# ScalarE evicts the second layer's state in unit 4s+4, ahead of squares and field copy, in place of unit 4s+5 (interaction network, one core, Trainium2)

## Chip, cores and metric

One Trainium2 chip, one core. The metric is the device time of one execution in microseconds (us). The engines named below are TensorE (PE: matmuls; PEld: its weight loads), VectorE (DVE), ScalarE (ACT), GpSimd (POOL) and SyncE (SP, which here only issues DMAs).

## What is computed

The kernel looks up 32 embeddings of 16 numbers for each of 2048 samples, passes them through three layers of a compressed interaction network, and puts the sums of the three layers and 16 dense numbers through a small MLP. Cut to what matters:

```python
e = stack([tbl_f[ids[:, f]] for f in range(32)], axis=1)          # (2048, 32, 16): x0
xk = x0
for W in (W0, W1, W2):                                            # (32, 32|64, 64)
    xk = relu(einsum('bmd,bhd,mhk->bkd', x0, xk, W))              # x1, x2, x3: (2048, 64, 16)
    outs.append(sum(xk, axis=2))
h = concatenate(outs + [dense_ctx], axis=1)                       # 208 wide
h = relu(h @ W_top1 + b_top1); h = relu(h @ W_top2 + b_top2)
y = h @ W_top3
```

## The kernel before, in words

**Blocks, pairs, units.** The 2048 x 16 pairs of sample and dimension are 32768 columns, cut into 64 blocks of 512 columns (s = 0 to 63). Two blocks make a pair (p = 0 to 31). Layers 1 and 2 of a block (from x1 to x2, and from x2 to x3) are contracted over 32 fields times 64 states, which is 16 matmul steps of 128 rows; four steps are one unit, so a block has four units, 4s to 4s+3, and a pair eight. An fp32 matmul stands in the trace as two instructions.

**The main loop.** Every engine runs the same loop, `for n in range(262)`, with four places i = 0 to 3 inside each n. In this document "unit n" is what an engine does for that n, and (n, i) is a place in it. The order of each engine's work is written out by hand and is fixed; engines meet through semaphores only, and each engine does its own list strictly in order.

- VectorE (`products`, line 637) makes at unit n first P1(n), the product of the loaded fields with x1 for layer 1, then P2(n-6), the product of the same fields with x2 for layer 2. P1 has three buffers, P2 two: P2(m) waits until TensorE has done P2(m-2), which is at TensorE's unit m+4. P2(4s), the first product of a block, also waits for x2 of block s (the semaphore `s_x[2]`). P2(4s) is made at VectorE's unit 4s+6.
- TensorE (`contract`, line 759, matmuls at L775) does at each place of unit n one step of P1(n) into the lower half of the array's columns and one of P2(n-6) into the upper half. Between the steps it does other work by tables: `sum_fields` (L698, L705) of the next pair into the one PSUM tile `wide`, `l0_tile` (L729), which multiplies the squares by the first layer's weights, `turn` (L681), which turns the next pair's fields round, and the MLP in `piece`s (L786, L795, L805).
- ScalarE evicts. `take_x2(s)` (line 476) waits for two things: TensorE's unit 4s+3 of layer 1, and P2(4s-1), the last reader of the x2 of the block before (`xp[2]` is one buffer). It then writes relu of the accumulator twice into `xp[2]` (L487, two instructions) and once into `zin` (L492). `square(p, t)` (line 444) squares what `sum_fields(p, t)` left in `wide` (L454); for t = 0 it first copies the fields (L452), and afterwards issues the DMA that stores them to DRAM (L458).
- SP (`keep_rows`, line 250) loads each unit's fields from DRAM, broadcast over partitions, into ten buffers `kept`; the loads of unit n wait for P2(n-10), and those of a pair also for its stored fields.

**The tables around the change.** For pairs from p = 3 on (p = 4 has two other places), the places are these, counted from unit 8(p-1):

```python
    SUMS_AT[later] = [(0, 2) if later == 4 else (0, 0), (1, 1), (2, 2), (4, 0), (4, 3)]
    L0_AT[later] = [(3, 0), (3, 2), (4, 2), (5, 0), (5, 2)]
```

So TensorE does the five tiles of field sums at (0,0), (1,1), (2,2), (4,0) and (4,3) of every eight units, and ScalarE has its squares of the same tiles at the same places of its list. There is one PSUM tile `wide` for all of them: `sum_fields(p, t)` waits (semaphore `s_took`) until ScalarE has squared tile t-1. At unit 8(p-1), ScalarE's list has, for t = 0, the copy of fields, the square and the store; then, at unit 8(p-1)+1, `take_x2` of an odd block, ahead of the square of t = 1. At unit 8(p-1)+4 it has the square of t = 3 at place 0 and that of t = 4 at place 3; then, at unit 8(p-1)+5, `take_x2` of an even block.

**MLP pieces.** Nine pieces for each group of four sample tiles are done at place 2 of units 79, 81, 87, 89, 95, 97, 103, 105, 111, then 64 units later, and again 64 units later; a last group is done near the end. Eight pieces of a group are eight matmul instructions each, the ninth is the small last layer.

Of the kernel before, what the change touches and what calls it, by code (L numbers as in the profile page):

```python
# [18 lines left out]
BLOCKS = B * D // BLK  # L19
# [6 lines left out]
UNITS = BLOCKS * GT  # L26
OFF = 6
# [24 lines left out]
def places(table):  # L52

    at = {}
    for p, where in table.items():
        for t, (o, i) in enumerate(where if isinstance(where, list) else [where]):
            at[8 * (p - 1) + o, i] = (p, t)
    return at


TURNS, SUMS, L0S, X1S = (places(table) for table in (TURN_AT, SUMS_AT, L0_AT, X1_AT))

SPLIT_AT = {1: (9, 10), 2: (4, 5)}
# [24 lines left out]
def halved(layer, s):  # L88

    return (layer, s) in ((1, 0), (2, BLOCKS - 1))  # L90


def tower(nc, dense_t, ids, tables, w_top1, b_top1, w_top2, b_top2, w_top3, w0_pairs, w0_all, w1, w2,
          sel_sums, identity, x0_rows, out):
    with ExitStack() as ctx:
# [299 lines left out]
        def _(act):  # L395
# [34 lines left out]
            def split_high(t):  # L430
                tile0 = M - EARLY if t % 2 == 0 else M
                act.wait_ge(s_gather[t % 2], 16 * (tile0 + M * (t // 2)))
                nc.scalar.copy(parts[:, :, 0, :], emb[t % 2][:, :, :].rearrange("p m d -> p d m"))\  # L433
                    .then_inc(s_high, 1)

            def split_mid(t):
                act.wait_ge(s_rest, t)
                nc.scalar.copy(parts[:, :, 1, :], rest[:, :, :]).then_inc(s_mid, 1)

            def take_x0(p):  # L440
                act.wait_ge(s_wide, 6 * (p - 1) + 1)
                nc.scalar.copy(x0[p % 2][:, :, :], wide[:, :, :]).then_inc(s_took, 1)  # L442

            def square(p, t):
                k = ST * p + t
                if k >= 2:
                    act.wait_ge(s_l0, k - 1)
                act.wait_ge(s_wide, 6 * (p - 1) + 2 + t)
                if t == 0:
                    if p >= 2:  # L450
                        act.wait_ge(s_stored[p % 2], 16 * (p // 2))
                    nc.scalar.copy(fields[p % 2], wide[0:M, :, :]).then_inc(s_fields, 1)  # L452
                n = 2 if t < ST - 1 else 1
                nc.scalar.activation(sq[k % 2][:, 0:n, :], wide[:, 0:n, :], ACT.Square).then_inc(s_took, 1)  # L454
                if t == 0:

                    act.wait_ge(s_fields, p)
                    act.dma_start(x0_rows[p].rearrange("j m n -> m j n"), fields[p % 2])\  # L458
                        .then_inc(s_stored[p % 2], 16)

            def take_x1(s):
                j = s % 2
                act.wait_ge(s_l0, ST * (s // 2 + 1))
                if s:
                    act.wait_ge(s_prod[1], 4 * s)
                src = acc0[64 * j:64 * j + 64, :]
                nc.scalar.activation(xp[1][0:64, :], src, ACT.Relu)  # L467
                nc.scalar.activation(xp[1][64:128, :], src, ACT.Relu).then_inc(s_x[1], 1)
                if s == 0:
                    for b in range(GT, rows):  # L470
                        keep_made(b)
                if s >= 6:
                    act.wait_ge(s_z12, (s - 6) // 4 + 1)
                nc.scalar.activation(zin[0:64, s % 6, :], src, ACT.Relu).then_inc(s_xz[1], 1)

            def take_x2(s):
                act.wait_ge(s_done[1], 4 * s + 4)
                if s:
                    act.wait_ge(s_prod[2], 4 * s)
                if halved(1, s):  # L480
                    src = [(accs[64 * c:64 * c + 64, s % 2, 0:HALF], slice(HALF * c, HALF * c + HALF))
                           for c in range(2)]
                else:
                    src = [(accs[0:64, s % 2, :], slice(0, BLK))]
                for half in range(2):
                    for bank, cols in src:
                        last = nc.scalar.activation(xp[2][64 * half:64 * half + 64, cols], bank, ACT.Relu)  # L487
                last.then_inc(s_x[2], 1)
                if s >= 6:
                    act.wait_ge(s_z12, (s - 6) // 4 + 1)  # L490
                for bank, cols in src:
                    last = nc.scalar.activation(zin[64:128, s % 6, cols], bank, ACT.Relu)  # L492
                last.then_inc(s_xz[2], 1)

            def take_x3(s):
                act.wait_ge(s_done[2], 4 * s + 4)
                if s >= 4:
                    act.wait_ge(s_z3, s // 4)
                if halved(2, s):
                    for c in range(2):  # L500
                        last = nc.scalar.activation(x3[:, s % 4, HALF * c:HALF * c + HALF],
                                                    accs[64 * c:64 * c + 64, s % 2, 0:HALF], ACT.Relu)
                else:
                    last = nc.scalar.activation(x3[:, s % 4, :], accs[64:128, s % 2, :], ACT.Relu)  # L504
                last.then_inc(s_xz[3], 1)

            def take_event(g, e):
                first, tiles = GROUPS[g]
                n = tiles * NB
                act.wait_ge(s_ev, 7 * g + e + 1)  # L510
                if e < 4:
                    nc.scalar.activation(h1[:, e, 0:n], exch[:, 0:n], ACT.Relu).then_inc(s_taken, 1)
                elif e < 6:
                    nc.scalar.activation(h2[:, e - 4, 0:n], exch[:, 0:n], ACT.Relu,
                                         bias=bt2[:, e - 4:e - 3]).then_inc(s_taken, 1)
                else:
                    nc.scalar.copy(y[:, first:first + tiles], exch[:, 0:tiles]).then_inc(s_taken, 1)
                if e == 3 and g + 2 < len(GROUPS):
                    load_dense(g + 2)
# [31 lines left out]
            for n in range(LAST):  # L551
                for i in range(GT):
                    t = n // 16 + 1
                    if i == 1 and t < BT and n % 16 == SPLIT_AT[t][0]:
                        split_high(t)
                    if i == 1 and t < BT and n % 16 == SPLIT_AT[t][1]:
                        split_mid(t)
                    if n % 4 == (OFF - 1) % 4 and i == 0 and 0 <= n - OFF + 1 < UNITS:
                        take_x2((n - OFF + 1) // 4)
                    if n % 4 == (OFF + 4) % 4 and i == 0 and n >= OFF + 4:  # L560
                        take_x3((n - OFF - 4) // 4)
                    if (n, i) in TURNS:
                        take_x0(TURNS[n, i][0])
                    if (n, i) in SUMS:
                        square(*SUMS[n, i])
                    if n % 8 == 2 and i == 0 and n + 2 < UNITS:
                        take_x1((n + 2) // 4)
                    if (n, i) in X1S:
                        take_x1(2 * X1S[n, i][0])
                    if (n, i) in PIECES_AT:  # L570
                        g, q = PIECES_AT[n, i]
                        if q < 4 or q == 8:
                            take_event(g, min(q, 6))
                        elif q % 2:
                            take_event(g, 4 + (q - 4) // 2)
# [367 lines left out]
```

## Time and profile before

| | |
|---|---|
| runs of the kernel before | 1278.5, 1280.6, 1282.85 us; median 1280.6 us |
| the profiled execution | span 1334.7 us from the first to the last instruction; the profile gives no other time of its own |
| TensorE busy | 92% of the span |
| VectorE busy | 86% |
| ScalarE busy | 39% |
| GpSimd busy | 51% |
| granted TensorE clock, mean | 0.990 of 2.4 GHz |

A row of a timeline gives the start in us from the span's start, the duration in us, engine, line, operation, output tile <- input tiles with partitions x elements and type, and how many instructions are merged. The bracket at the end is how long the engine was idle before the row and what released it. VectorE's and TensorE's instructions overlap a little with the next ones, so a product of 2.28 us duration is followed by the next 2.20 us after its start. In VectorE's rows, `prod<-kept,xp` is a P1 and `prod<-kept,xe` a P2 (x2 lies in the PSUM tile `xe`). In TensorE's rows, `prod,w1s` is layer 1 and `prod,w2s` layer 2.

### The profile page before, as it was taken

What the parts mean: (1) busy time and instruction counts of PE and PEld (TensorE: products, weight loads), DVE (VectorE), ACT (ScalarE), POOL (GpSimd) and SP (SyncE); (2) the same over time, 40 slices, a digit from 0 to 9 for tenths busy, and PEclk for the clock granted to TensorE, in tenths of its full rate; (3) what the DMA queues carried; (4) which work ended last, traced back from release to release, by engine and by line L of the source; (5) the groups of instructions that cost most, each with busy time, mean ns of one, the idle gap of its engine ahead of it and who ended that gap; (6) DMA issues with size and microseconds to landing.
All of it is one profiled execution on the core that took longest, in us unless ns stands there. A gap on an engine that the chain in (4) does not pass through costs nothing.

```text
span 1334.7 us, 16080 instructions
## 1 busy us (share of the span) xinstructions
PE 1233.3 (92%) x6140; PEld 507.4 (38%) x6140; DVE 1150.9 (86%) x534; ACT 517.9 (39%) x758; POOL 684.3 (51%) x705
## 2 busy tenths in 40 slices
PE   0779698999999999999999899999999999999998
PEld 0332233433444433333443333333444433333444
DVE  3259588989989899999998899999999999999994
ACT  0334143434434344444334344334434344434421
POOL 6553666674866556463745456374655652020201
PEclk9989899999999999999999999999999999999999
DMA  5348577997878788888899999999999988777850
GB/s 115 100 109 215 142 224 201 218 223 218 244 214 239 216 249 221 232 224 229 235 190 206 213 233 230 237 232 228 229 243 247 241 238 225 226 221 224 229 155 1
DMA packets 73547, 277.45 MB, mean 208 GB/s; under 512 B 29752, under 2 KB 38619, under 8 KB 41183
## 3 DMA queue, kind: packets, MB, share of 16 engines
q1 hardware_dynamic: 54324, 267.09, 77.3%
q0 software_dynamic: 16384, 4.23, 3.1%
q10 hardware_dynamic: 2762, 5.12, 1.5%
q8 instruction: 48, 0.79, 0.3%
q14 instruction: 29, 0.23, 0.1%
HBM read 272.15 MB, written 4.20 MB: 207 GB/s over the span
## 4 chain that ended last, share of the span: by engine, by line
PE 52%; DVE 15%; issue 12%; DMA 9%; another core or an unknown queue 4%; ACT 3%; POOL 2%; SPq 2%; DVEq 0%; ACTq 0%; POOLq 0%
PE accs L775 37%; DVE prod L649 15%; DMA kept<-x_rows 9%; PE acc L729 6%; PE wide L698 2%; POOL emb L293 2%; SPq L256 2%; PE xe L786 2%; PE xe L795 2%; ACT xe L487 1%; PE wide L681 1%; ACT sq L454 0%; PE accs L771 0%; ACT x3f L452 0%
## 5 line engine op out<-in xcount | busy, mean ns | idle before, releaser
L775 PE MATMUL accs<-prod,w2s 128*64 128x512 f32 x2016 | 950.6, 597 | 27.8 <-DVE prod L649 19.1
L775 PE MATMUL accs<-prod,w1s 128*64 128x512 f32 x2016 | 940.2, 596 | 0.0
L649 DVE TENSOR_TENSOR prod<-kept,xe 128x2048 f32<-128x2048 f32 x256 | 584.2, 2283 | 98.2 <-ACT xe L487 37.0
L293 POOL DMA_INDIRECT emb<-in_tbl,idx x512 | 485.9, 949 | 261.1 <-issue 123.0
L649 DVE TENSOR_TENSOR prod<-kept,xp 128x2048 f32<-128x2048 f32 x256 | 583.9, 2282 | 31.4 <-issue 13.8
L775 PEld LDWEIGHTS accs<-prod,w1s 128*64 128x64 f32 x2016 | 270.3, 137 | 266.4 <-issue 236.1
L775 PEld LDWEIGHTS accs<-prod,w2s 128*64 128x64 f32 x2016 | 266.1, 137 | 264.3 <-issue 185.0
L454 ACT ACTIVATE sq<-wide 128x1024 f32<-128x1024 f32 (+1 forms) x155 | 145.7, 940 | 310.4 <-PE wide L698 78.7
L729 PE MATMUL acc<-sq,u 128*64 128x512 f32 x640 | 234.1, 597 | 10.0 <-ACT sq L454 9.8
L698 PE MATMUL wide<-x,sums 128*64 128x512 bf16 x500 | 107.3, 384 | 11.7 <-issue 6.9
L332 POOL TENSOR_TENSOR x3f<-x3f 64x512 f32<-64x512 f32 x31 | 39.7, 1279 | 133.1 <-ACT x3f L504 132.9
L729 PEld LDWEIGHTS acc<-sq,u 128*64 128x64 f32 x640 | 67.4, 138 | 90.6 <-issue 71.9
L300 POOL TENSOR_TENSOR rest<-emb,parts 128x512 f32<-128x512 f32 x15 | 21.3, 1423 | 121.6 <-ACT parts L433 121.6
L487 ACT ACTIVATE xe<-accs 64x512 f32<-64x512 f32 (+1 forms) x130 | 73.1, 562 | 24.4 <-DVE prod L649 18.6
L312 POOL TENSOR_TENSOR zin<-zin 128x512 f32<-128x512 f32 x32 | 41.2, 1287 | 77.3 <-ACT zin L492 75.6
L504 ACT ACTIVATE x3f<-accs 64x512 f32<-64x512 f32 x63 | 37.5, 595 | 100.1 <-PE accs L775 74.9
L442 ACT CAST x<-wide 128x1024 bf16<-128x1024 f32 x31 | 31.4, 1012 | 103.2 <-PE wide L681 78.5
L698 PEld LDWEIGHTS wide<-x,sums 128*64 128x64 bf16 x500 | 39.9, 110 | 70.5 <-issue 59.5
L452 ACT COPY x3f<-wide 32x1024 f32<-32x1024 f32 x31 | 31.0, 1001 | 83.5 <-PE wide L698 57.6
L467 ACT ACTIVATE xp<-acc 64x512 f32<-64x512 f32 x64 | 36.4, 569 | 63.0 <-DVE prod L649 46.0
L842 PE MATMUL acc<-u 128*128 128x384 f32 x32 | 12.9, 564 | 35.6 <-DMA emb<-in_tbl,idx 35.6
L492 ACT ACTIVATE zin<-accs 64x512 f32<-64x512 f32 (+1 forms) x65 | 37.9, 584 | 1.6
(85 smaller groups left out, 463.1 us busy)
## 6 DMA issues: line engine op xcount, KB each, us to landing
kept<-x_rows SPq DMA_DIRECT2D x252, 512.0 KB
kept<-x_rows SPq DMA_DIRECT2D x504, 256.0 KB
emb<-in_tbl,idx POOLq DMA_INDIRECT x512
x_rows<-x3f ACTq DMA_DIRECT2D x31, 128.0 KB
prod<-in_w_all ACTq DMA_DIRECT2D x1, 512.0 KB, 6.2
w1s<-in_L_rec_W SPq DMA_DIRECT2D x4, 128.0 KB
w2s<-in_L_rec_W SPq DMA_DIRECT2D x4, 128.0 KB
wt<-in_W_top SPq DMA_DIRECT2D x1, 512.0 KB
```

The lines of the kernel that those rows point to most:

```text
L293: pool.indirect_dma_start(emb[t % 2][:, m, :], None, tables[m], bass.IndirectOffsetOnAxis(ap=idx[:, t, m:m + 1].bitcast(U32), axis=0)).the ...
L312: pool.tensor_tensor(zin[:, a, :], zin[:, a, :], zin[:, a + 1, :], ALU.add).then_inc(s_zp, 1)
L332: pool.tensor_tensor(x3[:, a, :], x3[:, a, :], x3[:, a + 1, :], ALU.add).then_inc(s_z3p, 1)
L454: nc.scalar.activation(sq[k % 2][:, 0:n, :], wide[:, 0:n, :], ACT.Square).then_inc(s_took, 1)
L467: nc.scalar.activation(xp[1][0:64, :], src, ACT.Relu)
L487: last = nc.scalar.activation(xp[2][64 * half:64 * half + 64, cols], bank, ACT.Relu)
L492: last = nc.scalar.activation(zin[64:128, s % 6, cols], bank, ACT.Relu)
L504: last = nc.scalar.activation(x3[:, s % 4, :], accs[64:128, s % 2, :], ACT.Relu)
L649: nc.vector.tensor_tensor(prod[layer][:, q % BUFS[layer], :, :], kept[:, q % KEPT, :, :], xp[layer][:, :].unsqueeze(1).to_broadcast([128, ...
L698: last = mm(bank[64 * c:64 * c + 64, :], sums[:, t, 64 * c:64 * c + 64], x0[p % 2][:, j, :], start=True, stop=True)
L729: last = mm(acc0[64 * j:64 * j + 64, :], w, squares, start=t == 0, stop=t == ST - 1)
L775: last = mm(accs[64 * (layer - 1):64 * layer, s % 2, :], wk[layer][:, t, :], prod[layer][:, q % BUFS[layer], i, :], start=t == 0, stop=t = ...
```

## The change

On ScalarE, `take_x2(s)` moves from place (4s+5, 0) to unit 4s+4: for an odd s to place 0, where it stands ahead of the copy of fields and the square of tile 0; for an even s to place 3, ahead of the square of tile 4 and behind that of tile 3. Nothing is added or taken away, and no other engine's list is touched.

```diff
+X2S = {(4 * s + 4, 0 if s % 2 else 3): s for s in range(BLOCKS)}
 TURNS, SUMS, L0S, X1S = (places(table) for table in (TURN_AT, SUMS_AT, L0_AT, X1_AT))
...
-                    if n % 4 == (OFF - 1) % 4 and i == 0 and 0 <= n - OFF + 1 < UNITS:
-                        take_x2((n - OFF + 1) // 4)
+                    if (n, i) in X2S:
+                        take_x2(X2S[n, i])
                     if n % 4 == (OFF + 4) % 4 and i == 0 and n >= OFF + 4:
                         take_x3((n - OFF - 4) // 4)
                     if (n, i) in TURNS:
```

## Rows read from the trace of the kernel before

**Rows 1.** The profile page, busy us (share of span) and instructions of two engines.

```profile
PE 1233.3 (92%) x6140; PEld 507.4 (38%) x6140; DVE 1150.9 (86%) x534; ACT 517.9 (39%) x758; POOL 684.3 (51%) x705
```

**Rows 2.** Groups by line, VectorE's P2: busy us, mean ns | idle before, by releaser.

```profile
L649 DVE TENSOR_TENSOR prod<-kept,xe 128x2048 f32<-128x2048 f32 x256 | 584.2, 2283 | 98.2 <-ACT xe L487 37.0 <-remote 27.3 <-issue 20.1
```

**Rows 3.** VectorE's timeline, a pair without MLP pieces: P2(112), P2(115), P2(117), P2(120).

```profile
651.91 2.29 DVE L649 TENSOR_TENSOR prod<-kept,xe 128x2048 f32<-128x2048 f32 x1 [1.27 <-issue]
...
665.11 2.28 DVE L649 TENSOR_TENSOR prod<-kept,xe 128x2048 f32<-128x2048 f32 x1
...
673.90 2.28 DVE L649 TENSOR_TENSOR prod<-kept,xe 128x2048 f32<-128x2048 f32 x1
...
688.44 2.29 DVE L649 TENSOR_TENSOR prod<-kept,xe 128x2048 f32<-128x2048 f32 x1 [1.27 <-issue]
```

**Rows 4.** ScalarE's timeline in the same pair, blocks 29 and 30.

```profile
664.63 1.00 ACT L452 COPY x3f<-wide 32x1024 f32<-32x1024 f32 x1 [2.45 <-issue]
665.65 1.02 ACT L454 ACTIVATE sq<-wide 128x1024 f32<-128x1024 f32 x1
...
667.48 1.15 ACT L487 ACTIVATE xe<-accs 64x512 f32<-64x512 f32 x2 [0.80 <-issue]
668.65 0.59 ACT L492 ACTIVATE zin<-accs 64x512 f32<-64x512 f32 x1
...
686.63 0.60 ACT L454 ACTIVATE sq<-wide 128x512 f32<-128x512 f32 x1 [2.62 <-PE wide L705]
687.25 1.15 ACT L487 ACTIVATE xe<-accs 64x512 f32<-64x512 f32 x2
```

**Rows 5.** VectorE's timeline, a pair with MLP pieces: P2(96), P2(101), P2(104).

```profile
577.28 2.29 DVE L649 TENSOR_TENSOR prod<-kept,xe 128x2048 f32<-128x2048 f32 x1 [2.28 <-ACT xe L487]
...
599.60 2.29 DVE L649 TENSOR_TENSOR prod<-kept,xe 128x2048 f32<-128x2048 f32 x1 [0.26 <-PE accs L775]
...
615.39 2.29 DVE L649 TENSOR_TENSOR prod<-kept,xe 128x2048 f32<-128x2048 f32 x1 [2.29 <-ACT xe L487]
```

**Rows 6.** TensorE's timeline, same pair: starts of units 104, 106, 110, 111, and work between.

```profile
589.91 0.59 PE L775 MATMUL accs<-prod,w1s 128*64 128x512 f32 x1
...
595.49 0.60 PE L698 MATMUL wide<-x,sums 128*64 128x512 bf16 x4
...
596.78 1.89 PE L795 MATMUL xe<-h,wt 128*64 128x512 f32 x8
598.50 0.59 PE L775 MATMUL accs<-prod,w1s 128*64 128x512 f32 x1
...
599.36 0.59 PE L775 MATMUL accs<-prod,w1s 128*64 128x512 f32 x1
...
618.46 0.59 PE L775 MATMUL accs<-prod,w1s 128*64 128x512 f32 x1
...
621.90 0.59 PE L775 MATMUL accs<-prod,w1s 128*64 128x512 f32 x1
622.12 0.64 PE L775 MATMUL accs<-prod,w2s 128*64 128x512 f32 x1
```

**Rows 7.** ScalarE's timeline near the start: a square that TensorE's field sums wait for.

```profile
87.15 1.02 ACT L454 ACTIVATE sq<-wide 128x1024 f32<-128x1024 f32 x1
```

**Rows 8.** TensorE's timeline, two early places: field sums that waited for a square.

```profile
88.23 0.62 PE L698 MATMUL wide<-x,sums 128*64 128x512 bf16 x4 [2.04 <-ACT sq L454]
...
228.00 0.64 PE L705 MATMUL wide<-x,sums 128*64 128x512 bf16 x2 [3.52 <-ACT sq L454]
```

**Rows 9.** TensorE's timeline, pair without pieces: field sums of tile 1.

```profile
668.41 0.59 PE L698 MATMUL wide<-x,sums 128*64 128x512 bf16 x2
```

**Rows 10.** Chain of waits, 655 to 700 us: a unit's loads on the path, start, us.

```profile
681.81 13.32 DMA kept<-x_rows
```

**Rows 11.** Stretches behind both waits: PE, PEld, DVE, ACT, POOL, granted clock, DMA.

```profile
88.30:92.00 3.70, 3.70 (x16) 1.33 (x17) 2.42 (x2) 1.03 (x1) 2.60 (x3) 1.00 0.50 95
227.50:231.00 3.50, 3.00 (x9) 1.34 (x11) 3.50 (x2) 2.65 (x5) 0.00 (x0) 0.51 0.19 70
```

## Prediction, made before the change was run

> **What bounds the kernel now.** I read the page's busy shares first: TensorE 1233.3 us and VectorE 1150.9 us of a 1334.7 us span [rows 1]. Two engines are nearly full, so a wait of one matters only where the other is not the bound at that moment. Then the groups by line: VectorE's idle time stands before its P2 products, 98.2 us, and the largest named releaser is the eviction of x2 (37.0 us) [rows 2]. Then the timelines, pair by pair, because the answer differs by stage.
>
> In a pair **without MLP pieces**, P2 of an even block starts late once per eight units: P2(112) and P2(120) each stand behind an idle of 1.27 us, 36.53 us apart [rows 3]. Between them VectorE is back to back: ten products from 651.91 to 673.90, 2.20 us each [rows 3]. Sixteen such products would be 35.2 us. The cause of the late one is on ScalarE: x2 of block 30 starts at 687.25, straight behind the square of tile 4 (686.63 and 0.60 long), and that square had waited for TensorE [rows 4]. The odd block shows no wait on VectorE, and its x2 had nothing to do with a square: after the square ended at 666.67 ScalarE stood idle 0.80 us and began x2 at 667.48, which is 0.09 after P2(115) ended (665.11 + 2.28) [rows 3, 4]. x2 of an odd block is released by P2(4s-1), and no place in the list can make it earlier.
>
> In a pair **with MLP pieces** the idle before P2(104) is 2.29 us, and P2(96) and P2(104) are 38.11 us apart [rows 5]. Here TensorE is the bound: its starts follow each other without a gap in its lower columns, and the only trace of VectorE's lateness is the upper half of unit 111, 0.22 us behind the lower (622.12 against 621.90) [rows 6]. A P2 even waits for TensorE, 0.26 us [rows 5].
>
> **The change part by part.** Three instructions of ScalarE (two relus to `xe`, one to `zin`) move; their number and durations stay. What counts is what stands behind what.
>
> *Even blocks: the gain.* x2 now stands behind the square of tile 3 and needs P2(4s-1) only; it is written while VectorE makes P1(4s+6), 2.20 us, and takes 0.09 + 1.15 us. The idle before P2(4s) goes: 1.27 us in a pair without pieces [rows 3]. The square of tile 4, now behind it, still waits for TensorE's sums (idle 2.62 before it) [rows 4], so it costs nothing; if that cover went, it would be late by 1.76 us. In a pair with pieces only the 0.22 us of rows 6 can come back; the rest of the 2.29 becomes waiting for TensorE.
>
> *Odd blocks: the cost.* x2 now stands ahead of the copy and square of tile 0, and it waits for P2(4s-1), in the middle of the unit. The copy, the square and the store's issue queue behind that wait, and TensorE's sums of tile 1 wait for the square. From the start of P2(4s-1): product 2.28, release 0.09, relus to x2 1.17, zin 0.62 (its 0.59 and the step to the next), copy 1.02, square 1.02 [rows 3, 4], release of TensorE 0.06 (88.17 to 88.23) [rows 7, 8]: **6.26 us**. In the pair of rows 3 that is 665.11 + 6.26 = 671.37, where TensorE did these sums at 668.41 [rows 9]: it stops for about 2.9 us the first time. The store is issued 4.6 us later; between its issue (behind the square at 665.65) and the next pair's first load (the loads on the chain begin to count at 681.81) there are now 15 us, then some 10. The trace shows no landing for it; the bounds are nothing and that of the far larger loads, 13.32 us [rows 10], which would make loads 3 us late per pair. I take nothing, as the store is an eighth of the bytes, and keep the other end as a small chance.
>
> *Pairs without pieces, summed.* The stop feeds the next wait. TensorE has, after the sums of tile 1, the rest of that unit and four units. By rows 6 the rest is 599.36 - 595.49 less the piece (598.50 - 596.78 = 1.72), 2.15, and units 106 to 109 are 618.46 - 599.36 = 19.10. Then VectorE's P2 that needs the last of them starts 0.24 later (599.60 against 599.36) [rows 5, 6], and four products at 2.20 lead to the next P2(4s-1). Round: 6.26 + 2.15 + 19.10 + 0.24 + 8.80 = **36.55 us**, against 36.53 now. The gain is all given back: VectorE no longer waits for ScalarE at P2(4s), but for TensorE at the P2s behind it. Bounds: 35.2, if TensorE made the stop up by itself, and 36.53 + 2.9, if nothing of the 1.27 helped.
>
> *Pairs with pieces, summed.* TensorE is the bound, and P2(4s-1) is released by the end of its unit 4s+3: start of unit 104 (589.91) + 0.24 + 6.26 = 596.41, against 595.49 now [rows 6]. It stops 0.92 us per pair and gets back 0.22: **+0.70 us**, 38.8 for 38.11. (The same round by VectorE, 36.55 + 1.72 = 38.27, is shorter, so TensorE's holds.) Bounds: -0.22 and +1.24, the latter if P2(4s-1) stays at VectorE's present pace.
>
> *Elsewhere.* In the first two pairs no square stands at the moved place; the end has no squares at all. Nothing.
>
> *Sum.* Of the pairs from p = 3 on, twelve are as rows 5 (three groups of pieces, four each): 12 x 0.70 = 8.4. Some sixteen are as rows 3: 16 x 0.02 = 0.3. Together about **+8.7 us**: the profiled execution 1334.7 to 1343.4, the median 1280.6 to 1289.3. The profiled execution is 54 us longer than the median; it has idle stretches in its first third with other releasers (27.3 us "remote" before P2 alone [rows 2]). I take the regular pairs as the common part and add the difference to the median: **1289 us**.
>
> **The clock.** The stop in pairs without pieces is in the steady round 36.55 less what TensorE needs: 38.11 - 0.22 - 2 x 1.72 = 34.45, so about 2.1 us. A wait of 2.04 us for a square left the granted clock at 1.00 (2.4 GHz); one of 3.52 us was followed by 3.5 us at 0.51, so near 1.2 GHz [rows 8, 11]. Ours lies with the first row, and I count nothing. The Trainium skill, "TensorE: Matmul & The Clock Gate", Part 1, says that the array falls to half clock after idling and earns the full one back by sustained work; the second row agrees. By that rule, if it bit here, the sum would be the one of the third rival below.
>
> **The rivals.**
> 1. *The gain stays* (faster). TensorE makes up the stop, and VectorE alone sets pairs without pieces: 16 x (36.53 - 35.2) = 21 us, and 12 x 0.22 = 3 with pieces: 1257 us. It decides at TensorE's sums of tile 1: if the square is taken by the time it gets there, or if TensorE has 2 us to spare per pair. For it: 36.53 - 34.45 = 2.1 us of room today, and 0.75 at 35.2. Against it: the stop falls in front of the units with the most extra work, and pieces leave no room. Half the gain would be about 1269. Chance 0.11.
> 2. *It cancels* (same). The stop in pairs with pieces is partly hidden, say a release to x2 before P2(4s-1)'s profiled end, or a zin and copy that overlap more: at 0.6 us less per pair 1282. Chance 0.15. That the change does nothing for odd blocks (their x2 cannot start earlier) is already in the sum.
> 3. *The clock falls* at the stops: a drop costs half of 3.5 us, 1.7; sixteen pairs: 27 more, 1316. Or late stores, 3 us in some pairs, toward 1310. For it: the first stop of 2.9 us lies between the two rows; against it: the steady one does not. Chance 0.07.
>
> **How the numbers follow.** The forecast (slower, about 1289) has 0.67. Its own range is 1284.5 to 1296: twelve pairs at up to 1.24, sixteen at up to 0.05 either way or a little over. A measurement of this kernel can tell about 0.3%, 3.8 us, from no change. The range that should hold 8 in 10 takes in the cancelling case and stops short of the gain and of the clock: 1279 to 1297. Slower 0.67 + 0.07 = 0.74; same 0.15; faster 0.11.
>
> **What would show it.** In the changed profile: no idle of 1.27 or 2.29 before P2 of even blocks; instead P2s that wait for TensorE by some tenths; TensorE idle before L698, released by the square L454, about 2 us in pairs without pieces and 0.9 with; x2 of odd blocks unmoved, 0.09 after P2(4s-1), then zin, copy and square in a row; pairs 36.5 and 38.8 us long. I am wrong if TensorE does not wait before L698, if pairs without pieces come out near 35.2, or if the granted clock shows 0.5 in the steady part.

## The result, and the profile after the change

The changed kernel takes 1301.86 us (median of four runs, 1300.65 to 1306.82) against 1281.72 us before (four runs, 1278.5 to 1282.92) in the same comparison: the ratio is 1.0167, 95% interval 1.0137 to 1.0198. It is slower by 20 us, where the forecast said 9 and its range ended at 1297. The direction held, the size did not.

The page of the changed kernel, then its P2 group and its P1 group (its lines stand one lower than before: L650 for L649, L699 for L698, L488 for L487):

```profile
PE 1212.2 (93%) x6140; PEld 438.1 (34%) x6140; DVE 1153.5 (88%) x534; ACT 515.8 (40%) x758; POOL 682.9 (52%) x705
```

```profile
L650 DVE TENSOR_TENSOR prod<-kept,xe 128x2048 f32<-128x2048 f32 x256 | 584.5, 2284 | 87.8 <-PE accs L776 77.7 <-ACT xe L488 7.1 <-issue 0.3
L650 DVE TENSOR_TENSOR prod<-kept,xp 128x2048 f32<-128x2048 f32 x256 | 583.5, 2281 | 10.5 <-ACT xp L469 10.5
```

Against [rows 2], the eviction of x2 no longer stands first among the releasers of P2; TensorE does, with 77.7 of 87.8 us. That is the exchange that the forecast described: the old wait is gone and another engine's lateness has its place.

The timeline of VectorE in two pairs without MLP pieces, to be held against [rows 3] (P2(112), P2(113), P2(115), P2(121), P2(129)):

```profile
620.55 2.29 DVE L650 TENSOR_TENSOR prod<-kept,xe 128x2048 f32<-128x2048 f32 x1 [0.31 <-PE accs L776]
...
625.84 2.29 DVE L650 TENSOR_TENSOR prod<-kept,xe 128x2048 f32<-128x2048 f32 x1 [0.81 <-PE accs L776]
...
634.64 2.28 DVE L650 TENSOR_TENSOR prod<-kept,xe 128x2048 f32<-128x2048 f32 x1
...
662.42 2.29 DVE L650 TENSOR_TENSOR prod<-kept,xe 128x2048 f32<-128x2048 f32 x1 [0.81 <-PE accs L776]
...
700.70 2.29 DVE L650 TENSOR_TENSOR prod<-kept,xe 128x2048 f32<-128x2048 f32 x1 [0.81 <-PE accs L776]
```

The idle of 1.27 before the even block's first product has become 0.31, released by TensorE, and P2(113) waits 0.81 more. From P2(113) to the same product of the next pair is 662.42 - 625.84 = 36.58 us.

ScalarE in that pair, against [rows 4], and TensorE's sums of tile 1, against [rows 9]:

```profile
637.02 1.15 ACT L488 ACTIVATE xe<-accs 64x512 f32<-64x512 f32 x2 [4.50 <-DVE prod L650]
638.19 0.59 ACT L493 ACTIVATE zin<-accs 64x512 f32<-64x512 f32 x1
638.80 1.00 ACT L453 COPY x3f<-wide 32x1024 f32<-32x1024 f32 x1
639.83 1.02 ACT L455 ACTIVATE sq<-wide 128x1024 f32<-128x1024 f32 x1
```

```profile
640.90 0.62 PE L699 MATMUL wide<-x,sums 128*64 128x512 bf16 x4 [1.98 <-ACT sq L455]
641.36 0.59 PE L776 MATMUL accs<-prod,w1s 128*64 128x512 f32 x1
...
677.48 0.76 PE L699 MATMUL wide<-x,sums 128*64 128x512 bf16 x4 [1.98 <-ACT sq L455]
678.02 1.06 PE L776 MATMUL accs<-prod,w1s 128*64 128x512 f32 x1
678.88 1.06 PE L776 MATMUL accs<-prod,w1s 128*64 128x512 f32 x1
```

ScalarE sits 4.50 us idle at x2 of the odd block, waiting for VectorE, with the copy and the square queued behind it. From the start of P2(115), 634.64, to TensorE's sums, 640.90, are 6.26 us, as in the forecast's chain. What the forecast did not count stands in the last rows. Two stops of the same 1.98 us, one pair apart, end differently: after the first the matmuls go on at 0.59 us, after the second they take 1.06. The view by stretches gives the granted clock behind the two stops (columns as in [rows 11]):

```profile
640.90:644.30 3.40, 3.40 (x18) 1.26 (x20) 3.40 (x3) 1.99 (x3) 1.85 (x3) 1.00 0.93 247
677.80:681.20 3.40, 3.40 (x12) 1.01 (x10) 2.29 (x2) 1.56 (x2) 2.38 (x2) 0.50 0.89 260
```

In 3.4 us TensorE starts 18 matmul instructions at 1.00 (2.4 GHz) and 12 at 0.50 (1.2 GHz). The pair with the fall takes 700.70 - 662.42 = 38.28 us, from P2(121) to P2(129), the one without 36.58: 1.7 us for one fall. Fifteen steady pairs have no pieces. In the three that follow a pair with pieces TensorE stops 1.05 us and the clock holds; of the other twelve stops, 1.98 us long and once 2.26, six ended with a fall: 6 x 1.7 = 10 us. One more stop, of 1.99 us at unit 17, ahead of the steady part, ended with a fall too.

A second place is units 24 to 31, where the places of pair p = 4 lie. ScalarE and TensorE there:

```profile
177.54 1.15 ACT L488 ACTIVATE xe<-accs 64x512 f32<-64x512 f32 x2 [8.90 <-DVE prod L650]
178.71 0.59 ACT L493 ACTIVATE zin<-accs 64x512 f32<-64x512 f32 x1
179.33 1.01 ACT L443 CAST x<-wide 128x1024 bf16<-128x1024 f32 x1
```

```profile
180.39 1.06 PE L699 MATMUL wide<-x,sums 128*64 128x512 bf16 x4 [3.79 <-ACT x L443]
181.25 1.06 PE L776 MATMUL accs<-prod,w1s 128*64 128x512 f32 x1
```

This pair is turned at (0,0), so under the change the copy of the turned fields (L443) stands behind x2 of block 5, which waits for P2(19). TensorE's first sums need that copy: it stops 3.79 us, and the clock is down when it goes on.

### The profile page after: what moved, and what is told of

Same layout as the page of the kernel before. It is cut to its first block, busy times and chain, and to the rows that moved or that the text cites. A ratio compares the mean times of both kernels' runs of the same rounds, so it can differ in the third digit from the quotient of the medians.

```text
span 1304.7 us, 16080 instructions
## 1 busy us (share of the span) xinstructions
PE 1212.2 (93%) x6140; PEld 438.1 (34%) x6140; DVE 1153.5 (88%) x534; ACT 515.8 (40%) x758; POOL 682.9 (52%) x705
## 4 chain that ended last, share of the span: by engine, by line
PE 63%; DVE 10%; ACT 7%; issue 6%; ACTq 0%
PE accs L776 45%; DVE prod L650 10%; PE acc L730 9%; PE wide L699 3%; PE xe L787 2%; ACT sq L455 2%; ACT x3f L453 2%; PE xe L796 2%; ACT xe L488 1%; ACT zin L493 1%; PE wide L682 1%; PE wide L706 0%; PE accs L772 0%; PE wide L796 0%; ACT x L443 0%
## 5 line engine op out<-in xcount | busy, mean ns | idle before, releaser
L776 PE MATMUL accs<-prod,w2s 128*64 128x512 f32 x2016 | 942.6, 601 | 2.2 <-DVE prod L650 2.2
L776 PE MATMUL accs<-prod,w1s 128*64 128x512 f32 x2016 | 942.2, 601 | 0.7 <-DVE prod L650 0.7
L650 DVE TENSOR_TENSOR prod<-kept,xe 128x2048 f32<-128x2048 f32 x256 | 584.5, 2284 | 87.8 <-PE accs L776 77.7
L650 DVE TENSOR_TENSOR prod<-kept,xp 128x2048 f32<-128x2048 f32 x256 | 583.5, 2281 | 10.5 <-ACT xp L469 10.5
L776 PEld LDWEIGHTS accs<-prod,w1s 128*64 128x64 f32 x2016 | 276.6, 139 | 497.3 <-issue 442.8
L776 PEld LDWEIGHTS accs<-prod,w2s 128*64 128x64 f32 x2016 | 275.3, 139 | 21.8 <-issue 10.0
L730 PE MATMUL acc<-sq,u 128*64 128x512 f32 x640 | 167.7, 596 | 3.3 <-ACT sq L455 3.1
L488 ACT ACTIVATE xe<-accs 64x512 f32<-64x512 f32 (+1 forms) x130 | 73.1, 562 | 149.7 <-DVE prod L650 143.2
L699 PE MATMUL wide<-x,sums 128*64 128x512 bf16 x500 | 79.2, 388 | 42.8 <-ACT sq L455 38.8
L730 PEld LDWEIGHTS acc<-sq,u 128*64 128x64 f32 x640 | 46.0, 137 | 93.2 <-issue 71.2
L443 ACT CAST x<-wide 128x1024 bf16<-128x1024 f32 x31 | 31.4, 1012 | 96.3 <-PE wide L682 96.3
L699 PEld LDWEIGHTS wide<-x,sums 128*64 128x64 bf16 x500 | 26.6, 110 | 126.6 <-ACT sq L455 64.4
L475 ACT ACTIVATE zin<-acc 64x512 f32<-64x512 f32 x64 | 37.3, 583 | 0.0
```

Source lines behind the costliest of these rows:

```text
L650: nc.vector.tensor_tensor(prod[layer][:, q % BUFS[layer], :, :], kept[:, q % KEPT, :, :], xp[layer][:, :].unsqueeze(1).to_broadcast([128, ...
L699: last = mm(bank[64 * c:64 * c + 64, :], sums[:, t, 64 * c:64 * c + 64], x0[p % 2][:, j, :], start=True, stop=True)
L730: last = mm(acc0[64 * j:64 * j + 64, :], w, squares, start=t == 0, stop=t == ST - 1)
L776: last = mm(accs[64 * (layer - 1):64 * layer, s % 2, :], wk[layer][:, t, :], prod[layer][:, q % BUFS[layer], i, :], start=t == 0, stop=t = ...
```

## The experiments

The theory after the result: the forecast's two rounds are right, and two costs come on top of them, the fall of the clock at some of the stops and the stop in units 24 to 31. The rivals are named with each run. Medians are of the kernel's own runs; ratios are those of the paired comparison, with their 95% intervals.

**The kernel before, profiled a second time.** No edit.

> The kernel before, unchanged, for a second profile. If the idle stretches that its first profile shows in the first third and at units 128 to 147 belong to that one execution, this profile's span is near 1285 us, with pairs of 36.53 and 38.11 us throughout. If they belong to the kernel, the span is again 1320 to 1335 us.

It ran in 1279.61 us; its span and clock, then its P2 group and P1 group:

```profile
core 0: 1277.8 us, clock 1.000
```

```profile
L649 DVE TENSOR_TENSOR prod<-kept,xe 128x2048 f32<-128x2048 f32 x256 | 583.9, 2281 | 63.3 <-ACT xe L487 55.0 <-PE accs L775 7.3
L649 DVE TENSOR_TENSOR prod<-kept,xp 128x2048 f32<-128x2048 f32 x256 | 583.5, 2281 | 13.3 <-ACT xp L468 6.8 <-DMA kept<-x_rows 4.1 <-issue 1.7
```

The releaser "remote" of [rows 2] is gone, and so are the long idle stretches: they belonged to that one execution, which was 54 us above the median. Pairs take 36.52 and 38.1 us, as read from the first profile, so the forecast's choice to carry the difference of the regular pairs over to the median was sound. This second profile is what the changed kernel has to be held against: 1304.7 - 1277.8 is 26.9 us. That is more than the 20 us of the medians, since the changed kernel's profiled run was the longest of its four (1306.82, at a clock of 0.986 where the other three have 0.989), and this one lies 3 us under the median of the kernel before in its comparison (1282.89).

**Only the even blocks moved.**

```diff
-X2S = {(4 * s + 4, 0 if s % 2 else 3): s for s in range(BLOCKS)}
+X2S = {(4 * s + 5, 0) if s % 2 else (4 * s + 4, 3): s for s in range(BLOCKS)}
```

> Only the even blocks' x2 is moved, the odd blocks' stays at unit 4s+5. My account (the odd blocks' move alone costs, the even blocks' gains): VectorE's idle of 1.27 before P2 of even blocks goes, nothing stops TensorE, pairs without pieces take 35.2 to 35.4 us in place of 36.53, pairs with pieces 37.85 in place of 38.11: sixteen times 1.2 and twelve times 0.25, about 22 us less than before, 1258 to 1263 us. The rival, that the loads of the fields hold VectorE as soon as it runs faster: P1 waits for the loads, and the time is within 8 us of before.

Measured: 1262.24 us (1260.5 to 1265.27, four runs), ratio to before 0.9849 (0.9818 to 0.988). VectorE's P2 and P1 groups, and two products 35.41 us apart in a pair without pieces:

```profile
L650 DVE TENSOR_TENSOR prod<-kept,xe 128x2048 f32<-128x2048 f32 x256 | 584.4, 2283 | 45.2 <-PE accs L776 31.6 <-ACT xe L488 11.1
L650 DVE TENSOR_TENSOR prod<-kept,xp 128x2048 f32<-128x2048 f32 x256 | 583.3, 2280 | 11.0 <-ACT xp L469 10.5 <-DMA kept<-x_rows 0.5
```

```profile
601.21 2.29 DVE L650 TENSOR_TENSOR prod<-kept,xe 128x2048 f32<-128x2048 f32 x1 [0.16 <-PE accs L776]
...
636.62 2.29 DVE L650 TENSOR_TENSOR prod<-kept,xe 128x2048 f32<-128x2048 f32 x1 [0.16 <-PE accs L776]
```

Pairs with pieces take 37.84. The even half of the change is worth about 20 us, and the loads do not hold the faster VectorE (0.5 us in all). This version is faster than both kernels.

**Only the odd blocks moved.**

```diff
-X2S = {(4 * s + 4, 0 if s % 2 else 3): s for s in range(BLOCKS)}
+X2S = {(4 * s + 4, 0) if s % 2 else (4 * s + 5, 0): s for s in range(BLOCKS)}
```

> Only the odd blocks' x2 is moved, the even blocks' stays behind the square of tile 4. My account: the round is 6.26 to the sums of tile 1, then 15.9 to the sums of tile 4, then 2.25 to P2 of the even block, then six products of 2.20: 37.6 us without pieces, 39.3 with: 1.1 and 1.2 us more than before per pair, and TensorE's stops are about 3 us, so that the clock falls more often (1.7 us each): 1315 to 1345 us. The rival, that moving the even blocks costs as well: then this one is faster than the change, under 1298 us.

Measured: 1318.02 us (1316.06 to 1318.88), ratio 1.0278 (1.0249 to 1.0306). Its P2 of an even block and TensorE's stop:

```profile
660.41 2.29 DVE L650 TENSOR_TENSOR prod<-kept,xe 128x2048 f32<-128x2048 f32 x1 [2.28 <-ACT xe L488]
```

```profile
679.87 0.62 PE L699 MATMUL wide<-x,sums 128*64 128x512 bf16 x4 [2.00 <-ACT sq L455]
680.32 0.59 PE L776 MATMUL accs<-prod,w1s 128*64 128x512 f32 x1
```

Pairs take 37.65 and 39.37 us, the round that was worked out beforehand (37.6 and 39.3). The odd half alone costs 36 us. One part of the expectation missed: the stops are not 3 us but 2.00, since TensorE comes to them later when the even blocks hold it too, and the clock fell at two of twelve (behind 2.00 us and behind the one of 2.27), not more often than in the change.

**Of the odd blocks, only the two relus ahead.** x2's third eviction (zin) is taken out of `take_x2` for odd blocks and stands at unit 4s+5, behind the square.

```diff
                 last.then_inc(s_x[2], 1)
+                if s % 2 == 0:
+                    take_z2(s)
...
+                    if n % 8 == 1 and i == 0 and n > 8:
+                        take_z2(n // 4 - 1)
```

> The change, but of an odd block only the two relus that VectorE reads stand ahead of the copy and the square of tile 0; the third (zin) stands behind them at unit 4s+5. My account: the square is 0.62 us earlier, and so is the whole round: 35.95 us without pieces, 38.15 with; TensorE's stop is about 1.4 us in place of 2.0 and does not bring the clock down: 1281.7 less 9, about 1272 to 1277 us, faster than before. If the stop's length does not set the time, it stays near the change's 1302 us; if the clock falls as often at 1.4 us as at 2.0, 1284 to 1290 us.

Measured: 1272.08 us (1269.15 to 1273.8), ratio 0.9915 (0.9885 to 0.9944). TensorE's stop (L710 and L787 here are L699 and L776 of the change):

```profile
622.16 0.62 PE L710 MATMUL wide<-x,sums 128*64 128x512 bf16 x4 [1.37 <-ACT sq L455]
622.62 0.59 PE L787 MATMUL accs<-prod,w1s 128*64 128x512 f32 x1
```

Pairs take 35.97 and 38.18 us: one eviction of 0.62 us on the chain is worth 0.6 us in every pair, and stops of 1.37 (once 1.65) never brought the clock down in the steady part. The chain from P2(4s-1) to the sums sets the round, as the theory has it.

**The stop filled.** In TensorE's list, ahead of the sums of tile 1 in pairs without a piece in flight, stand twelve matmuls whose result nobody reads:

```diff
+            def keep_busy(n):
...
+                for k in range(6):
+                    for c in range(2):
+                        mm(exch[64 * c:64 * c + 64, :], sums[:, 0, 64 * c:64 * c + 64],
+                           x0[(n // 8 + 1) % 2][:, 0, :], start=True, stop=True)
...
+                    if n % 8 == 1 and i == 1 and 17 <= n < UNITS - 8 and quiet(n):
+                        keep_busy(n)
```

> The change, and in TensorE's list, ahead of the sums of tile 1 in the thirteen or so pairs that have no MLP piece in flight, twelve spare matmuls of the form of the field sums into a PSUM tile that nobody reads then: 1.29 us of work inside a stop of 1.98. They can't move the sums, which wait for the square in any case. My theory (stops of 1.98 us bring the clock down in some of the pairs, 1.7 us each, six times in the profile): the granted clock stays at 1.00 at those places, every pair without pieces takes 36.6 us, and the time is 5 to 10 us under the change's: 1291 to 1297 us. The rival, that the pairs of 38.27 us have another cause (a late store or load): they stay, and the time is 1300 to 1304 us.

Measured: 1293.46 us (1290.51 to 1296.62, ten runs), ratio 1.0096 (1.0074 to 1.0118). The spare matmuls, the rest of the stop, and the clock behind it:

```profile
628.33 1.47 PE L843 MATMUL xe<-x,sums 128*64 128x512 bf16 x12
630.48 0.62 PE L699 MATMUL wide<-x,sums 128*64 128x512 bf16 x4 [0.69 <-ACT sq L455]
```

```profile
630.50:633.90 3.40, 3.40 (x18) 1.25 (x20) 3.40 (x3) 2.00 (x3) 1.86 (x3) 1.00 0.90 266
```

No pair takes 38.27 us any more; all without pieces are at 36.58 to 36.86. TensorE does more work in the same places and the kernel is 8.4 us faster than the change. This shows that the falls of the clock made the longer pairs; the rival, a late store or load, would have left them.

**Block 5 put back.**

```diff
-X2S = {(4 * s + 4, 0 if s % 2 else 3): s for s in range(BLOCKS)}
+X2S = {(25, 0) if s == 5 else (4 * s + 4, 0 if s % 2 else 3): s for s in range(BLOCKS)}
```

> The change, with block 5 alone left where it was. Its pair (p = 4) has its turn at (0,0) and its first sums at (0,2), so that under the change the copy of x0 stands behind x2 of block 5, which waits for P2(19), and TensorE stops 3.79 us for the copy. My theory: that stop goes, units 24 to 31 take 37 to 38 us in place of 41.5, and the time is 4 to 6 us under the change's, 1296 to 1298 us. The rival, that this place is hidden behind late gathers at units 16 to 24: 1300 to 1303 us.

Measured: 1297.09 us (1294.36 to 1300.71, ten runs), ratio 1.0097 (1.0063 to 1.0132): 4.8 us under the change. TensorE's stop of 3.79 for the copy is gone, while the clock still falls behind six of the twelve steady stops. P2(17) and P2(25), in the change and then here:

```profile
166.37 2.29 DVE L650 TENSOR_TENSOR prod<-kept,xe 128x2048 f32<-128x2048 f32 x1 [0.20 <-PE accs L776]
...
207.84 2.29 DVE L650 TENSOR_TENSOR prod<-kept,xe 128x2048 f32<-128x2048 f32 x1 [0.81 <-PE accs L776]
```

```profile
163.86 2.28 DVE L650 TENSOR_TENSOR prod<-kept,xe 128x2048 f32<-128x2048 f32 x1
...
200.08 2.29 DVE L650 TENSOR_TENSOR prod<-kept,xe 128x2048 f32<-128x2048 f32 x1 [0.16 <-PE accs L776]
```

That stretch takes 41.47 us in the change and 36.22 here, 5.25 less.

**Both.** The edits of the two runs before, in one kernel.

> Both of the runs before in one kernel. What is left is the two rounds of the forecast: 12 pairs at +0.70 and 16 at +0.05 over the kernel before, 9 us. My theory: 1288 to 1293 us. If the two parts hide one another, 1294 to 1298 us.

Measured: 1288.09 us (1284.51 to 1290.59, ten runs) against 1281.43 before (25 runs, 1277.42 to 1296.63) in the same comparison; the paired ratio is 1.0015 (0.9983 to 1.0046), so by the ratio alone what is left can't be told from nothing. The profiles tell it: the span is

```profile
core 0: 1286.6 us, clock 0.999
```

against 1277.8, 8.8 us more, at the same clock, and its pairs take 36.58 and 38.79 us where the kernel before has 36.52 and 38.1.

These three runs were timed in the same comparison, so their medians can be subtracted: from both edits (1288.1) the clock's falls are 1297.1 - 1288.1 = 9.0 us, block 5 is 1293.5 - 1288.1 = 5.4, and the rounds 1288.1 - 1281.4 = 6.7. Together 21.1, where the change measured 20.1. The split is good to some us only: by the paired ratios it is 10.5, 10.4 and 1.9 us, the last with an interval that ends at 5.9, while the pairs of the two profiles give the rounds 12 x 0.68 + 15 x 0.06 = 9 us. The traces bear out 5 us for block 5 and about 10 for six falls.

## Why the prediction was right in its direction and wrong in its size

- *Even blocks: the gain.* Right. The idle before P2 of even blocks went, and alone the move gives 20 us, near the 24 of the first rival, which needed just this: a TensorE that isn't stopped.
- *Odd blocks: the cost.* Right to the hundredth: 6.26 us from P2(4s-1) to the sums.
- *Pairs without pieces.* 36.55 forecast, 36.58 measured. The stop was put at 2.1 us and shows as 1.98 of idle (the next step says why these agree). There are fifteen such steady pairs, not sixteen. The gain is given back in full, through TensorE.
- *Pairs with pieces.* 38.8 forecast, 38.79 measured. The stop of 0.92 was forecast as a delay of the sums' start; the trace counts 0.76 of idle from the end of the matmul before:

```profile
564.67 0.59 PE L776 MATMUL accs<-prod,w1s 128*64 128x512 f32 x1
...
566.03 0.62 PE L699 MATMUL wide<-x,sums 128*64 128x512 bf16 x4 [0.76 <-ACT sq L455]
```

  That matmul lasts 0.59, where without a stop the next one starts 0.43 behind it. From start to start the delay is 566.03 - 564.67 - 0.43 = 0.93, as forecast, and 0.93 - 0.68 = 0.25 comes back, near the 0.22 that was credited.
- *The store.* Right to be left out: in the changed kernel VectorE's P1 waits for no load at all, only for x1 (10.5 us), and its profile page puts the store's median landing at 3.8 us from the issue, within the 10 us of room.
- *Elsewhere.* **Wrong.** The step says that nothing happens outside the regular pairs, but pair p = 4 is turned at (0,0), in the very place where x2 of block 5 now stands. The places were in the tables; the step looked only for squares at the moved place, not for the copy that they depend on. It costs about 5 us.
- *The clock.* **Wrong, and by the medians the larger part.** The step set the stop of 2.1 us beside one row with 2.04 us and a clock that held, and counted nothing. One row that held is no bound: the same stop holds in half of the pairs and lets the clock fall in the other half. Nor was that row like the steady part, where TensorE runs at 1.00 up to the stop. Ahead of its wait the clock had only just risen (columns as in [rows 11]):

```profile
80.00:83.00 3.00, 2.88 (x14) 1.58 (x16) 1.72 (x1) 1.72 (x4) 2.08 (x4) 0.50 0.08 6
83.00:86.10 3.10, 3.10 (x18) 1.39 (x14) 0.57 (x1) 0.00 (x0) 0.78 (x1) 0.81 0.09 5
```

  The third rival named the mechanism and the price (1.7 us each, right) but gave it sixteen falls or none, and 0.07; it came in six steady pairs, about 9 us. With both terms the sum is 8.7 + 9 + 5.4 = 23, against 20; the 3 us between them are within what the split above leaves open.

## What to carry to other kernels

On an engine that works its list in order, moving an eviction earlier also moves its wait in front of everything behind it: ask first what releases it. Here the odd blocks' x2 was held by its reader, so that the move could win nothing for it and cost the squares behind it 4.6 us. Where a move is made by a rule for all blocks, look at it by parity and by the exceptions of the tables, since one half was worth 20 us and the other cost more than that; and where TensorE is given a new stop of about 2 us, price the fall of its clock as a share of the stops, not as all or none.

## What the runs showed that was not expected

TensorE's granted clock fell to 0.50 behind stops of only 1.98 us, in six of twelve pairs of the change (and again in six of twelve with block 5 put back), in two of twelve with only the odd blocks moved (eleven stops of 2.00 and one of 2.27), and in none of the steady ones at 1.37 or with the stop filled down to 0.69. Nor does the longest stop decide: the one of 2.27 was followed by a fall, the one of 2.26 in the change was not. So the length of the stop alone doesn't decide; what picks the pairs was not tried and stays open. The Trainium skill, "TensorE: Matmul & The Clock Gate", section "HAM oscillation", warns of idle gaps longer than these and reckons the loss as half of the throttled time. The runs agree on the loss (1.7 us for 3.4 us at 0.50) and differ on the gap, and the measurement decides.

Filling a stop with work whose result nobody reads made the kernel faster, 1293.5 against 1301.9 us, because it kept the clock at 1.00; taking the stop away, as in the version with the even blocks alone, is worth far more.
